# Splitting each score step of an attention stage by token tile, with other matrix products between the parts

## What is computed

```
s0, s1 = relu(x @ swi[j]) @ swo[j]               # two shared experts, 128 -> 512 -> 128
x  = eo * w[:, 0] + s0 * w[:, 1] + s1 * w[:, 2]   # eo: the expert of the row's type
h  = layernorm(x)
q, k, v = split(h @ w_qkv + b_qkv)                # 16 heads of 8
scores  = q k^T / sqrt(8)                         # within each batch of 32 tokens
o  = softmax(scores) @ v
x  = x + o @ w_o + b_o
h  = layernorm(x)
top 2 of 8 experts by h @ gate_w, 128 -> 512 -> 128, weighted and added to x
```

## Time and profile before

| | |
|---|---|
| median of 3 runs | 684.29 us (683.05 to 684.35) |
| the profiled execution | 685.2 us, of which the profile's span is 683.4 us |
| TensorE busy | 82% of the span |
| VectorE, ScalarE, GpSimd busy | 59%, 56%, 49% |
| mean granted TensorE clock | 0.928 of full speed |
| score MATMULs | the first starts at 305.3, the last at 495.9 us |

### The profile page before, as it was taken

The page is one execution under the profiler, slowest core; times in us unless marked ns, Lnnn a source line. Parts: engine busy times, 40 slices in busy tenths (PEclk is TensorE's granted clock), DMA queues, the critical chain, the costliest instruction groups (busy, mean ns, idle before and its releaser), DMA issues. The chain is left out here.

```text
span 683.4 us, 18201 instructions
## 1 busy us (share of the span) xinstructions
PE 563.6 (82%) x5428; PEld 433.8 (63%) x5429; DVE 403.1 (59%) x1407; ACT 383.1 (56%) x792; POOL 333.3 (49%) x372
## 2 busy tenths in 40 slices
PE   1578999866699992999999999898988929999950
PEld 1233555434699991666666666566778829999950
DVE  6235888994433321045767777768777554655636
ACT  0225767775466631457466566565756707888830
POOL 1236477774100002343456767665558734777750
PEclk9998999995799996899999999998999977999995
DMA  8920011111622210010533221213312222222229
GB/s 274 316 40 1 15 36 39 36 62 58 186 64 69 62 28 4 16 44 21 158 77 139 64 63 34 56 48 73 72 45 71 69 67 61 73 72 72 72 60 341
DMA packets 72071, 54.03 MB, mean 79 GB/s; under 512 B 25816, under 2 KB 63520, under 8 KB 71600
## 3 DMA queue, kind: packets, MB, share of 16 engines
q1 hardware_dynamic: 60400, 34.36, 18.3%
q0 software_dynamic: 6432, 13.25, 6.0%
q10 hardware_dynamic: 5152, 5.34, 2.4%
HBM read 30.30 MB, written 22.62 MB: 77 GB/s over the span
## 5 line engine op out<-in xcount | busy, mean ns | idle before, releaser
L1309 POOL DMA_INDIRECT rows_dram<-u_row,u_slots x64 | 62.6, 978 | 38.9 <-DVE u_slots L2192 22.3
L1446 PE MATMUL u_py<-u_hh,cwo 128*128 128x512 f32 x128 | 64.1, 595 | 0.0
L2474 POOL DMA_INDIRECT y_dram<-x_y,x_to x48 | 48.2, 1003 | 27.3 <-DVE x_y L2580 26.5
L1797 ACT ACTIVATE u_hh<-u_pz 128x512 f32<-128x512 f32 x64 | 36.7, 596 | 36.4 <-PE u_pz L1438 36.1
L2510 PE MATMUL x_py<-w,x_h 128*128 x384 | 51.6, 278 | 0.1
L2569 DVE TENSOR_SCALAR x_h<-x_pc,p_bT 128x128 f32<-128x128 f32 x96 | 29.5, 347 | 36.2 <-PE x_pc L2500 35.9
L2510 PEld LDWEIGHTS x_py<-w,x_h 128*128 128x128 f32 x384 | 47.6, 195 | 0.3 <-issue 0.3
L1263 POOL DMA_INDIRECT u_eo<-eo_dram,type_slot x1 | 1.0, 1027 | 84.7 <-issue 84.7
L2539 ACT ACTIVATE x_held_w<-w 128x512 f32 x48 | 30.2, 630 | 19.4 <-PEq L1217 12.8
L788 POOL DMA_INDIRECT xs_dram<-x,type_slot x32 | 31.6, 987 | 17.8 <-DVE x L702 10.0
L953 PE MATMUL e_py<-cwt,e_h 128*128 x288 | 38.5, 277 | 0.9 <-issue 0.7
(11 more groups left out here) (370 smaller groups left out, 1640.0 us busy)
## 6 DMA issues: line engine op xcount, KB each, us to landing
w<-in_mw SPq DMA_DIRECT2D x2, 2048.0 KB, 8.4
x_xs<-rows_dram SPq DMA_DIRECT2D x48, 65.0 KB
cwt<-in_cw SPq DMA_DIRECT2D x1, 2560.0 KB, 10.4
xs_dram<-zero SPq DMA_DIRECT2D x1, 2304.0 KB, 16.6
e_xs<-xs_dram SPq DMA_DIRECT2D x36, 64.0 KB, 1.9
eo_dram<-e_y SPq DMA_DIRECT2D x36, 64.0 KB, 1.6
x_dram<-x SPq DMA_DIRECT2D x8, 256.0 KB, 2.0
x1t<-x_dram SPq DMA_DIRECT2D x8, 256.0 KB, 4.7
```

Source lines behind the costliest of these rows:

```text
L1309: pool.indirect_dma_start(rows_dram, bass.IndirectOffsetOnAxis(ap=slots[:, q, k, u:u + 1], axis=0), row[:, q, k, u, :], None).then_inc(sen ...
L1446: nc.tensor.matmul(py[:], cwo[:, m * KF + k], hh[:, e % HR], start=(m == 0 and k == 0), stop=(m == NSH - 1 and k == KF - 1)).then_inc(s_ma ...
L1797: act.activation(hh[:, e % HR], pz[e % 2][:], ACT.Relu).then_inc(hh_made, 1)
L2474: pool.indirect_dma_start(y_dram, bass.IndirectOffsetOnAxis(ap=to[t % R][:], axis=0), y[:, t % R, :], None).then_inc(sent[t % R], 16)
```

## The change

`scores` takes the tile `u` as a third argument and emits only the 8 products of that tile. The waits for `u_qT`, `u_km` and the two banks stand ahead of the part for tile 0, and `scored` is signalled by the part for tile 3. In the loop other steps stand between the parts; behind the loop the four parts follow each other as before. Only TensorE's list changes.

```
-                def scores(i, h):
-                    pe.wait_ge(qT_made, i + 1)
-                    pe.wait_ge(km_made, i + 1)
-                    claim("g0")
-                    claim("g1")
-                    for u in range(SB):
-                        for b in range(BT):
+                def scores(i, h, u):
+                    if u == 0:
+                        pe.wait_ge(qT_made, i + 1)
+                        pe.wait_ge(km_made, i + 1)
+                        claim("g0")
+                        claim("g1")
+                    for b in range(BT):
...
+                    if u == SB - 1:
+                        last.then_inc(scored, 1)
...
                     if ok(i - 2):
-                        scores(i - 2, 1)
+                        scores(i - 2, 1, 0)
                     if ok(i):
                         first(i, 1, 0)
+                    if ok(i - 2):
+                        scores(i - 2, 1, 1)
                     if ok(i - 3):
                         turn_h(i - 3)
                     if ok(i):
                         first(i, 1, 1)
+                    if ok(i - 2):
+                        scores(i - 2, 1, 2)
                     if ok(i - 3):
                         logits(i - 3)
                     if ok(i - 1):
                         turn_normed(i - 1)
                     if ok(i):
                         second(i, 0, 3)
+                    if ok(i - 2):
+                        scores(i - 2, 1, 3)
                     if ok(i - 1):
                         query(i - 1)
...
                     if ok(i - 1):
-                        scores(i - 1, 0)
+                        scores(i - 1, 0, 0)
                     if ok(i + 1):
                         first(i + 1, 0, 0)
+                    if ok(i - 1):
+                        scores(i - 1, 0, 1)
                     if ok(i):
                         second(i, 1, 3)
+                    if ok(i - 1):
+                        scores(i - 1, 0, 2)
                     if ok(i + 1):
                         first(i + 1, 0, 1)
+                    if ok(i - 1):
+                        scores(i - 1, 0, 3)
...
-                scores(NB - 2, 1)
+                for u in range(SB):
+                    scores(NB - 2, 1, u)
```

More of the change, by code:

```diff
@@ L1484, in value_rows @@
                     free["e"] = (vtok_made, i + 1)
-                def scores(i, h):
-                    pe.wait_ge(qT_made, i + 1)
-                    pe.wait_ge(km_made, i + 1)
-                    claim("g0")
-                    claim("g1")
-                    for u in range(SB):
-                        for b in range(BT):
[L1493 to L1498, removed]
+                def scores(i, h, u):
[5 more added lines that the diff above has]
+                    for b in range(BT):
+                        t = slice((u * BT + b) * S, (u * BT + b + 1) * S)
+                        for g in (2 * h, 2 * h + 1):
+                            r = slice(g * GW, (g + 1) * GW)
+                            last = nc.tensor.matmul(pgh[g % 2][b * S:(b + 1) * S, u * P:(u + 1) * P], qT[r, t], km[r, :, t],
+                                                    start=True, stop=True)
+                    if u == SB - 1:
+                        last.then_inc(scored, 1)
                 def turn_p(i, g):
@@ L1694, in _ @@
                 turn_row(4)
-                scores(NB - 1, 0)
+                for u in range(SB):
+                    scores(NB - 1, 0, u)
                 turn_o(NB - 2)
@@ L1704, in _ @@
                 second_row(3)
-                scores(NB - 1, 1)
+                for u in range(SB):
+                    scores(NB - 1, 1, u)
                 first_row(5)
```

## The result

The changed kernel takes 710.63 us (median of 4 runs, 708.03 to 714.37) against 684.32 (median of 4): 26.3 us more, ratio 1.038 with a 95% interval of 1.033 to 1.044. The prediction was 711.5, range 697 to 727. The profiled execution is the slowest of the four, 714.37 us, with a span of 712.7.

The account below looks back on a forecast made before the run. PE was taken to bound the loop. Six full A (11.7), six B (14.7) and the last A (0.35 plus 0.25) total 27.0 us, on 685.2 or 684.29, giving 711.5 us, range 697 to 727.

Parts of the forecast that it names:

- What bounds the loop: In the loop PE alone is full, busy 25.89 of 26.00 us; what lengthens its stream lengthens the kernel equally.
- Price of a gap: On PE, each extra part of a score step pays again for going in and coming out: 0.35 us, bounds 0.30 and 0.40.
- A: First-half score step, scores(i-1, 0), in seven loop iterations; six full ones were put at 1.95 us each, 11.7 together.
- B: Second-half score step, scores(i-2, 1), in six loop iterations; put at 2.45 us each, 14.7 together.
- three gaps: +1.05 per step: On PE, a score step split into four parts has three gaps, which add 1.05 us to the step.
- Step A's late signal: VectorE's maxima and mix end later, so turn_x waits for its bank: 0.9 us of waiting besides 1.05 of gaps.
- Step B's late signal: PE waits at turn_p(2) some 1.2 us, then at attend: 1.4 of waiting plus 1.05 of gaps, 2.45 us.
- The last A: At i = 7, two pairs with one gap: 0.35 us plus a guess of 0.25 for its late signal.
- Gaps only: Rival, chance 0.12: in the loop late signals hide and only the gaps cost, 13 us, giving 697.
- late signals only: Rival, chance 0.07: PE's loads run ahead across the shape change, gaps are free, waits cost 14 us, giving 698.
- The clock falls as well: Rival, chance 0.10: PE's waits lower its granted clock, 3.2 us per fall, 19 over six blocks, giving 731.
- Faster: Rival, chance 0.05: products between parts let PE's instruction supply refill; 13 in-loop steps lose 0.40 each, 5.2 us, giving 679.

Follow-up runs that it names:

- the early gaps: Against the kernel before: the same four parts per in-loop score step, but between products that stood ahead of the step; 693.04 us, ratio 1.0145.
- the halves: Against the changed kernel: each in-loop score step in two parts of two tiles, the second behind the first product that follows; 688.19 us, ratio 1.008.
- the late whole step: Against the changed kernel: both in-loop score steps undivided, each where its fourth part stands; 707.59 us, ratio 1.034 to the kernel before.

## Why the prediction was right, step by step

**What bounds the loop.** Right: all that was added to PE's stream, or that PE waited for, is in the time.

**Price of a gap.** Put at 0.35, with 0.30 and 0.40 as bounds; in A it measured 0.35: the product behind A's last part has its second MATMUL at 371.65, so its slot begins at 371.65 - 0.23 = 371.42, 4.48 behind A's start, against 385.62 - 382.18 = 3.44 in the earlier trace rows, hence 1.04 for three. A product behind small ones thus starts 0.11 ahead of its slot (383.26 against 383.37 in the prediction), and with that B's three gaps cost only (384.15 + 0.11 - 378.13) - (396.84 - 391.42) = 6.13 - 5.42 = 0.71, or 0.24 each. One reason can be read from the loads of logits, before and after (two fences, one kernel each):

```profile
394.60 0.97 PEld L1551 LDWEIGHTS u_pf<-p_gwm,u_hT 128*128 128x128 f32 x8 [0.42 <-ACT u_hT L1841]
```

```profile
381.44 0.97 PEld L1552 LDWEIGHTS u_pf<-p_gwm,u_hT 128*128 128x128 f32 x8 [0.20 <-issue]
```

In the kernel before logits waited for u_hT: its first MATMUL stood at 394.60, 0.39 behind the start of the one ahead of it and not 0.23. The part that now stands ahead of it covers these 0.16, about half of the 0.34 by which B came out lower; the other half is open. The term "three gaps: +1.05 per step" was right for A and 0.34 too high for B. A price of 0.29 over both kinds of place came out of the changed kernel (1.75 for six), the early gaps and the halves alike.

**Step A's late signal.** Right to 0.1 us. With A's start as the common point (366.94 in this block, 382.18 in the prediction's, 15.24 apart), mix began at 374.15 where I had it at 374.21, and turn_x was entered at 375.42 where I had 375.46. One wait was not put: turn_p(0) stood for u_p before that (the load at 373.63, idle for 0.89), and from the L1446 ahead of it (372.55) to the L1436 behind it (374.21) PE took 1.66, where it had taken 387.96 - 386.74 = 1.22. So 0.44 of the 0.91 were waited off there, and only the rest at turn_x. The sum is the same, since mix sets when turn_x starts. No wait for u_xl, as put; the late whole step shows that this hung on the part ahead of it. VectorE in the changed kernel:

```profile
371.50 0.69 DVE L2114 TENSOR_REDUCE u_mx<-u_pg 128x16 f32<-128x512 f32 x1 [3.48 <-PE u_pg L1496]
...
374.15 1.11 DVE L2078 SCALAR_TENSOR_TENSOR u_cres<-u_eo,u_wtok,u_turns 128x128 f32<-128x128 f32 x4
...
384.33 0.69 DVE L2114 TENSOR_REDUCE u_mx<-u_pg 128x16 f32<-128x512 f32 x1 [4.28 <-PE u_pg L1496]
```

**Step B's late signal.** The shift was right, 2.45, by two errors that cancel. From query to attend PE needs 389.67 - 384.26 = 5.41 against 3.67: 1.74 of waiting, where I had 1.4. The step that failed is the list of what stands behind the maxima. I named gate, but followed only its way to counts; it also frees the bank that keys takes, and keys stood 0.19 us on u_lb (387.31). The gaps, put at 1.05, measured 0.71, so PE entered query 0.34 sooner than put and waited it off again; attend began at 389.67, where my 404.9 gives 389.66. ScalarE in that stretch:

```profile
388.12 0.68 ACT L1828 ACTIVATE u_qT<-u_pe,p_bqk 128x512 f32<-128x512 f32 x1
388.88 0.60 ACT L1847 ACTIVATE u_ptT<-u_pg 128x512 f32<-128x512 f32 x1
```

Between u_qT and the last u_ptT there are 0.08 us. So without the wait for u_lb attend could have begun hardly sooner, and PE would have stood ahead of it; the missing release changed where PE waited more than how long. No run takes it out. That attend agrees to 0.01 is partly luck: this last copy ended at 389.48, 0.2 ahead of the 404.9 that I had put for it.

**Ends.** The last A: put at +0.6. From it to the next score step the profiled executions take 502.00 - 492.96 = 9.04 and 471.34 - 462.83 = 8.51, so +0.5. Behind that the changed kernel wins 1.4, and ahead of the loop it loses 1.0; neither has a cause that was looked for.

**The rivals.** *Gaps only* and *late signals only* are refuted by the runs with one of them each, and by the waits in the trace. *The clock falls as well*: once in the loop of the profiled execution, at a price of about 1.5 us, not in each block. *Faster*: refuted: each gap costs, and the idle loads behind a part are the same 0.20 for 16, 32 and 64 products. On the other chips whole steps of 64 did come in pieces (50, 5, 6, 3), as that rival would have it. A's split alone cost 1.012 there, 8.7 us, where the theory put 12; whether whole steps in pieces are the reason stays open, since the interval of that ratio, 1.005 to 1.020, holds the theory's 1.018 as well.

## What to carry to other kernels

A step that changes the array's shape has a price at its two ends, here 0.3 us together for each part of 16 or 32 products; keep it whole. A step whose result others wait for should not be stretched over time: its signal comes with its last part. And follow every release behind the delayed instruction to the bank or buffer it frees, not only to its obvious reader; a gap on the engine that bounds the kernel can hide a wait, so costs measured one at a time do not add up.

## What the runs showed of the hardware

- 32x32 products of f32 start every 0.014 us on average when eight corners are in use. The turn from 32x32 to 128x128 work leaves the weight loads idle for 0.20 us, behind 16, 32 and 64 products alike, where no semaphore wait adds to it.
- The same kernel takes 683 us on one chip and 740 and 738 on two others. The traces from those two show stops of PE, VectorE and ScalarE for nothing that the profile shows, and in one of them a dense run of small products comes to 5 or 6 every 0.72 us after the first 50.
- With the kernel before at 683 to 684 us, a stop of PE of 2.6 us was followed by a fall of the clock to 1.2 GHz in two kernels (PE busy for 6.3 of the 7.4 us ahead of it) and not in three others (the kernel before, the early gaps, the halves; 7.4 of 7.4).
